# Contiguous one-hot tables, and the weight splits of two experts laid between the row fetches

## Chip, cores and metric

The kernel runs on one core of a Trainium2 chip. The metric is the time of one execution on the device, in microseconds (us). The time before is the median of three runs, 1259.48 us.

## The reference

Two layers run on x of shape (4, 1024, 256), 4096 tokens of 256 features. Each layer is `x = layernorm(x + attention(x))` and then `x = layernorm(x + ffn(x))`. The change touches the last ffn only, a mixture of eight experts of which each token takes two, plus one shared expert:

```python
T = B * S                                   # 4096 tokens, H = 256, D = 512, E = 8
scores = softmax(xt @ Wr)
topk_w, topk_idx = top_k(scores, 2)
topk_w = topk_w / (topk_w.sum(-1, keepdims=True) + 1e-20)
g = silu(einsum('th,ehd->etd', xt, Wg))
u = einsum('th,ehd->etd', xt, Wu)
out_all = einsum('etd,edh->eth', g * u, Wd)
out = sum(out_all[topk_idx, tok] * topk_w[..., None], axis=1)
shared = silu(x @ Sg) * (x @ Su) @ Sd
return out + shared
```

## The kernel before

Matrix products run in pairs of fp32r operands: each fp32 matrix is split in a high part and the rest (low), and a product is three matmuls (function `three`, L1681 to L1683). Each engine's program is written out by hand, with semaphores between them.

The expert stage begins once the tokens are normed. The order of its work is this.

**Routing.** VectorE works out the two experts of each token and, for each of its two places, a slot in a table sorted by expert. The slots form 71 tiles of 128 rows (NE = 71). By the reference's inputs the eight experts take 9, 6, 8, 9, 10, 7, 7 and 12 tiles, so expert 2 begins at tile 15, expert 3 at tile 23, expert 4 at tile 32 and expert 5 at tile 42; three tiles at the end are empty.

**The token table.** Which token stands in slot (tile n, row r) is found by 64 small matmuls (`token_table`, L1993), one for each of 32 blocks of 128 tokens and each of the two places. The stationary operand `in_row` is a one-hot over the 128 rows, the moving operand `in_tile` a one-hot over the 71 tiles, scaled by the token's number. Both are fp16 and are laid out with the block index innermost, eight to a group, so each operand is read at a step of eight elements. VectorE builds `in_tile` (L1549) and `in_row` in four quarters (L1564); ScalarE scales `in_tile` block by block, 32 instructions (L683), each of which releases two matmuls. Between the halves of the table TensorE runs pieces of `down_wide` (L2003), the down projection of the first two chunks of the shared expert. VectorE turns the sums into `token_of` (L1579), and that starts GpSimd.

**GpSimd's queue (L943 to L964).** GpSimd fetches the rows of the first six tiles straight to where TensorE needs them, asks for expert 2's weights (`load_expert(2)`), and fetches the rows of the other 65 tiles in 17 groups. Group 0 is tiles 6 and 7, every other group four tiles (the last three). A `fetch` (L913) is one indirect DMA of 128 rows of 1 KB into one of six stage buffers; `keep` (L920) writes a whole group to DRAM (`tokens_by_expert`), from where ScalarE's queue loads a tile three tiles ahead (L727). Between groups GpSimd splits the weights of experts 2 and 3: `split_expert` copies 128x3072 elements to the high part (L908), drains, and subtracts for the low part (L910), which releases `w_ready`. Slots for weights are three: `load_expert(e)` with e of 3 and more waits until expert e-3 is done with (L935).

**The tile loop.** For each tile TensorE transposes the rows (L2038), runs gate and up (24 matmuls of EWs with xeh, xel), transposes the hidden rows (L2054, four matmuls), and runs down (heh, hel). ScalarE does Silu (L718) and the high parts (L713, L723), VectorE the product (L1625), the low parts (L1619, L1629) and the copy out (L1637), SyncE the store. A tile waits for its rows and, by `w_ready`, for its expert's split weights (L2076).

**The end.** GpSimd gathers the experts' outputs for each token by 64 indirect DMAs (L969), while TensorE runs the other six chunks of the shared expert; then come the last sums and norms.

Of the kernel before, what the change touches and what calls it, by code (L numbers as in the profile page):

```python
# [16 lines left out]
TB = N // P  # L17
KD = D // P
# [8 lines left out]
ROUND = 12582912.0  # L27


C_ID, C_IOTA, C_CAUSAL, C_CHAN = 0, 128, 640, 896  # L30
# [3 lines left out]
C_TOKEN = 1192  # L34
# [14 lines left out]
STAGES = 6  # L49
SLOTS = 3  # L50
AHEAD = 2
# [15 lines left out]
def wait(eng, sem, n):  # L67

    if not isinstance(n, int) or n > 0:
        eng.wait_ge(sem, n)  # L70
# [12 lines left out]
def build(nc, cst, xT, x, wqkvgT, wave_cols, bias_cols, coupling_rows, woutT, bout, wgu_rows, wd_rows, wqk_T, wo_rows, bo, wr, experts, out):  # L83
    ctx = ExitStack()
    with ctx:
        place = {"at": 0, "top": 0}

        def sb(name, shape, dt=F32):
            size = 2 if dt in (BF16, F16) else 4
            for s in shape[1:]:  # L90
                size *= s
            t = nc.alloc_sbuf_tensor_at(name, shape, dt, offset=base + place["at"])
            place["at"] += (size + 31) // 32 * 32
            place["top"] = max(place["top"], place["at"])
            return t

        def sem(name):
            return ctx.enter_context(nc.semaphore(name))
# [3 lines left out]
        PS = ctx.enter_context(nc.psum_tensor("PS", [P, 8, 512], F32))  # L102
# [3 lines left out]
        C = sb("C", [P, C_END])  # L106
# [4 lines left out]
        zrow = sb("zrow", [P, D])  # L111
# [121 lines left out]
        place["at"] = kept  # L233
        in_tile = sb("in_tile", [P, 2, NT // 8, NE, 8], F16)
        inc_ = sb("inc_", [P, NT, E])
# [21 lines left out]
        place["at"] = slot_at + 4 * SLOT  # L257
        in_row = sb("in_row", [P, NT // 8, 2, P, 8], F16)
        posf, tilef = sb("posf", [P, 2, NT]), sb("tilef", [P, 2, NT])
        tile_of, row_of = sb("tile_of", [P, 2, NT], F16), sb("row_of", [P, 2, NT], F16)  # L260
        bigt = sb("bigt", [P, NE + 1, E])
        past, third = sb("past", [P, NE + 1]), sb("third", [P, NE + 1])
        columns = sb("columns", [P, P, 8], F16)
        sco, oh1 = sb("sco", [P, NT, E]), sb("oh1", [P, NT, E])
        assert place["at"] <= slot_at + 8 * SLOT

# [11 lines left out]
        d_gr = [sem("d_gathered" + str(i)) for i in range(NCH)]  # L278
        x_kept, d_tile, d_row, d_token, d_table, d_token_of, d_stage0, d_stage1, d_rows, d_row0, d_row1, d_last = (
            sem("d_" + n) for n in ("x_kept", "tile", "row", "token", "table", "token_of", "stage0", "stage1", "rows", "row0", "row1", "last"))  # L280
        d_stage = (d_stage0, d_stage1)
# [95 lines left out]
        def _(act):  # L377
# [385 lines left out]
        def _(pool):  # L763
# [141 lines left out]
            def split_expert(e):  # L905
# [90 lines left out]
        def _(dve):  # L996
# [447 lines left out]

            dve.tensor_copy(columns[:], C[:, C_IOTA:C_IOTA + P].unsqueeze(2).to_broadcast([P, P, 8]))
            dve.tensor_copy(tri[:], C[:, C_TRI:C_TRI + P])
# [88 lines left out]
            for j, oh in enumerate((oh1, oh2)):  # L1535
                dve.tensor_tensor(tmp[:], slot[:], oh[:], ALU.mult)
                dve.drain()
                dve.tensor_reduce(posf[:, j], tmp[:], AX.X, ALU.add)
                dve.drain()
            dve.tensor_copy(pos[:], posf[:])  # L1540

# [3 lines left out]
            dve.drain()  # L1545
            dve.tensor_scalar(tile_of[:], tilef[:], ROUND, ROUND, ALU.add, ALU.subtract)
            dve.drain()
            dve.scalar_tensor_tensor(row_of[:], tile_of[:], -float(P), posf[:], ALU.mult, ALU.add)
            dve.tensor_tensor(in_tile[:].rearrange("p j q n t -> p (j q) n t"),  # L1549
                              columns[:, 0:NE].unsqueeze(1).to_broadcast([P, NT // 4, NE, 8]),  # L1550
                              tile_of[:].rearrange("p j (q t) -> p (j q) t", t=8).unsqueeze(2).to_broadcast([P, NT // 4, NE, 8]),
                              ALU.is_equal).then_inc(d_tile, 1)
            hidden(1, 2)
            dve.drain()
            def added(c):
                for w in range(2):
                    dve.wait_ge(d_dn, 2 * c + w + 1)
                    rows = X[:, 4 * c + 2 * w:4 * c + 2 * w + 2]
                    src = PS[:, 6 + w].rearrange("p (t d) -> p t d", d=D)
# [8 lines left out]
            added(0)  # L1568
            dve.tensor_scalar(past[:], past[:], float(E - 1), None, ALU.min)
# [8 lines left out]
            dve.wait_ge(d_table, 1)  # L1578
            dve.tensor_scalar(token_of[:], PS[:, 0, 0:NE], float(TOKEN_0), None, ALU.add).then_inc(d_token_of, 1)  # L1579

            def gated(c, part):
# [96 lines left out]
        def _(pe):  # L1678
# [307 lines left out]

            def token_table(first, end):
                for t in range(first, end):
                    pe.wait_ge(d_token, t + 1)
                    if t % (NT // 4) == 0:  # L1990
                        pe.wait_ge(d_row, 4 * t // NT + 1)
                    for j in range(2):
                        mm = pe.matmul(PS[:, 0, 0:NE], in_row[:, t // 8, j, :, t % 8], in_tile[:, j, t // 8, :, t % 8], start=t + j == 0, stop=t + j == NT)  # L1993
                if end == NT:
                    mm.then_inc(d_table, 1)

            def down_wide(c, first, end):
                wait(pe, d_add, 2 * c)
                pe.wait_ge(d_ld, 32)
                for j in range(first, end):  # L2000
                    pe.wait_ge(d_hb, 4 * c + j + 1)
                    for w in range(4):
                        mm = pe.matmul(PS[:, 6 + w // 2, (w % 2) * D:(w % 2 + 1) * D], inner[c][:, j, w * P:(w + 1) * P],  # L2003
                                       wide_down[:, j * D:(j + 1) * D], start=j == 0 and w % 2 == 0, stop=j == 3 and w % 2 == 1)
                        if j == 3 and w % 2:
                            mm.then_inc(d_dn, 1)
# [196 lines left out]
```

## Time and profile before

| | |
|---|---|
| median of 3 runs | 1259.48 us (1257.24 to 1261.27) |
| the profiled execution, its time | 1258.39 us |
| its span in the trace | 1256.2 us |
| TensorE busy | 1068.5 us (85%) |
| VectorE busy | 791.2 us (63%) |
| ScalarE busy | 480.7 us (38%) |
| GpSimd busy | 442.8 us (35%) |

A row of the profile names the line, the engine (PE is TensorE, PEld its weight load, DVE VectorE, ACT ScalarE, POOL GpSimd), the operation, out<-in and the shape. In square brackets is how long the engine stood still before it and what released it. "issue" means that the trace shows nothing that it waited for; "remote" means a queue that the trace does not know. The profiled execution's time lies 2.2 us above its span and 1.1 us below the median.

### The profile page before, as it was taken

The page shows a single profiled execution, that of the slowest core. Times are in us where ns is not written, and L with a number is a line of the kernel's source. Part 1 is how long each engine was busy: PE and PEld are TensorE (multiplying, and loading weights), DVE is VectorE, ACT ScalarE, POOL GpSimd, SP SyncE. Part 2 cuts the span into 40 slices and gives each one's busy share as a digit, 9 for nine tenths or more (in the row PEclk, how much of TensorE's full clock was granted, in tenths as well). Part 3 has the DMA queues.
Part 4 walks back from the last instruction along what each step waited for, and adds up shares of the span by engine and source line. Part 5 has one row for each costly group of instructions (what it writes and reads, how often), then busy time and mean ns, then how long its engine had stood idle before and what let it go on. Part 6 is the DMA issues. An engine that isn't in the chain of part 4 may idle for free.

```text
span 1256.2 us, 19144 instructions
## 1 busy us (share of the span) xinstructions
PE 1068.5 (85%) x5944; PEld 923.8 (74%) x5945; DVE 791.2 (63%) x1337; ACT 480.7 (38%) x813; POOL 442.8 (35%) x387
## 2 busy tenths in 40 slices
PE   5699953599999999999899858699999999832995
PEld 4567733589999998999777747588888888711884
DVE  7978898799999985887652313244444444301887
ACT  6635532234444445667471212123222223200345
POOL 3202003145544454231106767644403000474032
PEclk9989985799999999999999879799999999955998
DMA  6100100000000002112404363651321111232122
GB/s 263 49 20 1 35 41 30 0 2 1 0 0 0 1 1 105 35 34 82 154 1 160 107 225 108 204 159 53 104 100 50 54 54 63 89 104 71 34 85 117
DMA packets 41203, 87.80 MB, mean 70 GB/s; under 512 B 5954, under 2 KB 27716, under 8 KB 39748
## 3 DMA queue, kind: packets, MB, share of 16 engines
q0 software_dynamic: 9696, 35.66, 9.2%
q1 hardware_dynamic: 20660, 39.20, 8.7%
q10 hardware_dynamic: 10800, 12.32, 3.2%
q8 instruction: 28, 0.46, 0.2%
q14 instruction: 19, 0.16, 0.0%
HBM read 57.80 MB, written 29.36 MB: 69 GB/s over the span
## 4 chain that ended last, share of the span: by engine, by line
PE 53%; DVE 15%; DVEq 9%; issue 8%; another core or an unknown queue 8%; ACT 4%; POOL 1%; POOLq 1%; DMA 0%; ACTq 0%
PE PS L1681 14%; PE PS L1683 13%; PE PS L1682 13%; PE PS L2054 3%; PE PS L1805 2%; DVEq L1184 2%; DVEq L1289 2%; ACT in_tile L683 2%; PE PS L1710 2%; DVEq L1301 1%; DVEq L1197 1%; DVE hx L1196 1%; PE PS L2038 1%; PE PS L1723 1%
## 5 line engine op out<-in xcount | busy, mean ns | idle before, releaser
L1625 DVE TENSOR_TENSOR hb<-PS,gs 128x512 f32<-128x512 f32 x71 | 49.1, 691 | 169.1 <-ACT gs L718 155.3
L1681 PE MATMUL PS<-EWs,xeh 128*128 x284 | 122.0, 430 | 1.5 <-DVE xel L1619 1.2
L1682 PE MATMUL PS<-EWs,xeh 128*128 x284 | 114.1, 402 | 0.0
L1683 PE MATMUL PS<-EWs,xel 128*128 x284 | 113.8, 401 | 0.0
L969 POOL DMA_INDIRECT gathered<-expert_outputs,pos x64 | 61.6, 963 | 145.4 <-DMA expert_outputs<-ye 126.1
L718 ACT ACTIVATE gs<-PS 128x512 f32<-128x512 f32 x71 | 42.4, 598 | 177.0 <-PE PS L1683 150.4
L1681 PE MATMUL PS<-WGh,bxh 128*128 128x352 f32 x256 | 88.4, 345 | 19.8 <-DVE hv L1283 13.5
L1681 PE MATMUL PS<-EWs,heh 128*128 x284 | 87.6, 308 | 18.1 <-DVE hel L1629 14.1
L1805 PE MATMUL PS<-WD,htf 128*128 128x256 f32 x384 | 88.5, 380 | 1.6 <-ACT htf L509 1.5
L723 ACT ACTIVATE heh<-PS 128x512 fp32r<-128x512 f32 x71 | 42.5, 598 | 123.2 <-PE PS L2054 90.4
L1682 PE MATMUL PS<-WGl,bxh 128*128 128x352 f32 x256 | 85.6, 334 | 0.0
L1683 PE MATMUL PS<-WGh,bxl 128*128 128x352 f32 x256 | 85.3, 333 | 0.0
L1629 DVE TENSOR_TENSOR hel<-PS,heh 128x512 fp32r<-128x512 f32 x71 | 49.1, 692 | 55.7 <-ACT heh L723 52.5
L1682 PE MATMUL PS<-EWs,heh 128*128 x284 | 81.7, 288 | 0.0
L1683 PE MATMUL PS<-EWs,hel 128*128 x284 | 81.5, 287 | 0.0
L1805 PEld LDWEIGHTS PS<-WD,htf 128*128 128x128 f32 x384 | 71.2, 190 | 10.9 <-ACT htf L509 2.5
L1681 PE MATMUL PS<-DTh,SWh 128*128 128x512 f32 x128 | 53.5, 418 | 20.2 <-issue 13.8
L1681 PE MATMUL PS<-xh,WQh 128*128 128x512 f32 x128 | 53.8, 420 | 19.8 <-DVE WQl L1019 13.2
L1681 PEld LDWEIGHTS PS<-EWs,heh 128*128 128x128 f32 x284 | 55.1, 194 | 19.6 <-issue 19.5
L1681 PEld LDWEIGHTS PS<-EWs,xeh 128*128 128x128 f32 x284 | 55.3, 195 | 17.9 <-issue 2.3
L1681 PEld LDWEIGHTS PS<-WGh,bxh 128*128 128x128 f32 x256 | 50.5, 197 | 23.6 <-issue 14.7
L1683 PE MATMUL PS<-DTh,SWl 128*128 128x512 f32 x128 | 52.4, 409 | 13.8 <-issue 13.8
(359 smaller groups left out, 3063.7 us busy)
## 6 DMA issues: line engine op xcount, KB each, us to landing
raw_of<-experts POOLq DMA_DIRECT2D x6, 1536.0 KB
expert_outputs<-ye SPq DMA_DIRECT2D x71, 128.0 KB
xe<-tokens_by_expert ACTq DMA_DIRECT2D x65, 128.0 KB
xraw<-xT SPq DMA_DIRECT2D x8, 512.0 KB, 5.6
X<-x SPq DMA_DIRECT2D x1, 4096.0 KB, 16.9
tokens<-X SPq DMA_DIRECT2D x8, 512.0 KB, 3.1
y<-X SPq DMA_DIRECT2D x8, 512.0 KB, 2.6
raw_of<-experts SPq DMA_DIRECT2D x2, 1536.0 KB, 9.1
```

The lines of the kernel that those rows point to most:

```text
L683: act.activation(of_t, of_t, ACT.Copy, scale=C[:, C_TOKEN + t:C_TOKEN + t + 1]).then_inc(d_token, 1)
L718: act.activation(gs[:, h], PS[:, 2], ACT.Silu).then_inc(e_si, 1)
L723: act.activation(heh[:, h].rearrange("p a c -> p (a c)"), PS[:, 4 + h], ACT.Copy).then_inc(e_hhi, 1)
L969: pool.indirect_dma_start(out=gathered[c][:, j, t], out_offset=None, in_=YS, in_offset=bass.IndirectOffsetOnAxis(ap=pos[:, j, 4 * c + t:4 ...
L1184: dve.drain()
L1625: dve.tensor_tensor(hb[:, h], PS[:, 3], gs[:, h], ALU.mult).then_inc(e_hb, 1)
L1629: dve.tensor_tensor(hel[:, h].rearrange("p a c -> p (a c)"), PS[:, 4 + h], heh[:, h].rearrange("p a c -> p (a c)").bitcast(F32), ALU.subtr ...
L1681: pe.matmul(out_, wh, vh, start=first, stop=False)
L1682: pe.matmul(out_, wh, vl, start=False, stop=False)
L1683: return pe.matmul(out_, wl, vh, start=False, stop=last_)
L1805: mm = pe.matmul(PS[:, 7, i * D:(i + 1) * D], htf[:, i, k], WD[:, k], start=k == 0, stop=k == FT - 1)
L2054: t = pe.transpose(PS[:, 4 + h, j * P:(j + 1) * P], hb[:, h, j * P:(j + 1) * P], ident)
```

## The change

The tables become contiguous: `in_tile` is [block, place, tile] with 72 columns in place of 71, and `in_row` is [block, place, row]. To keep pairs of equal elements side by side, `tile_of` and `row_of` are written twice each, and the comparison reads the iota row in pairs. ScalarE's 32 scalings go; VectorE multiplies the whole `in_tile` by the token numbers in one instruction ahead of `in_row`. `token_table` runs in one piece between `down_wide(0)` and `down_wide(1)`, which gets banks of its own (4 and 5), and VectorE's `added(0)` moves behind `token_of`.

On GpSimd, the splits of experts 2 and 3 are cut in six column ranges of 512 elements, high and low part each, twelve pieces in all. A piece stands behind every second fetch of groups 2 to 7 (expert 2) and 9 to 14 (expert 3); each low piece has a drain of its own ahead of it. The wait for expert 2's raw weights moves ahead of group 2, the load of expert 3 stays behind group 7, and group 8 goes between it and the wait for it. The splits of experts 4 to 7 stay whole.

```diff
+            def split_part(e, n):
+                place_, half, cols = (e + 2) % SLOTS, n % 2, slice(n // 2 * 2 * D, (n // 2 + 1) * 2 * D)
+                hi, lo, raw = (t[:, cols].rearrange("p (n d) -> p n d", d=D) for t in (hi_of[place_], lo_of[place_], raw_of[place_]))
+                if half == 0:
+                    pool.tensor_tensor(hi, raw, zrow[:, :].unsqueeze(1).to_broadcast([P, 2, D]), ALU.add)
+                else:
+                    pool.drain()
+                    last_ = pool.tensor_tensor(lo, raw, hi.bitcast(F32), ALU.subtract)
+                    if n == PARTS - 1:
+                        last_.then_inc(w_ready, 1)
...
-            def gather_tokens(first, end):
+            def gather_tokens(first, end, split=None):
+                part = 0
                 for g in range(first, end):
...
                     for n, i in enumerate(range(*GROUPS[g])):
                         fetch(stages[g % STAGES][:, n], i, d_stage[g % 2])
+                        if split is not None and n % 2:
+                            split_part(split, part)
+                            part += 1
...
             gather_tokens(0, 2)
             pool.wait_ge(d_dn, 2 * AHEAD)
-            gather_tokens(2, 4)
-            loaded(2)
-            gather_tokens(4, 8)
+            pool.wait_ge(d_raw2, 16)
+            gather_tokens(2, 8, split=2)
             load_expert(3)
-            gather_tokens(8, 10)
-            loaded(3)
-            gather_tokens(10, 16)
+            gather_tokens(8, 9)
+            pool.wait_ge(d_raw2, 16 * 2)
+            gather_tokens(9, 15, split=3)
+            gather_tokens(15, 16)
             load_expert(4)
...
-            act.wait_ge(d_tile, 1)
-            for t in range(NT):
-                of_t = in_tile[:, :, t // 8, :, t % 8]
-                act.activation(of_t, of_t, ACT.Copy, scale=C[:, C_TOKEN + t:C_TOKEN + t + 1]).then_inc(d_token, 1)
...
+            dve.tensor_tensor(each_tile, pairs(columns[:, 0:NE + 1], 2 * NT), doubled(tile_of[:], (NE + 1) // 2), ALU.is_equal)
             hidden(1, 2)
             dve.drain()
+            dve.tensor_tensor(each_tile, each_tile, doubled(tokens[:].rearrange("p t (j d) -> p t j d", d=2), (NE + 1) // 2),
+                              ALU.mult).then_inc(d_tile, 1)
...
-                dve.tensor_tensor(in_row[:, q], columns[:].unsqueeze(1).to_broadcast([P, 2, P, 8]),
-                                  row_of[:, :, 8 * q:8 * q + 8].unsqueeze(2).to_broadcast([P, 2, P, 8]), ALU.is_equal).then_inc(d_row, 1)
+                dve.tensor_tensor(in_row[:, 8 * q:8 * q + 8].rearrange("p t j (n d) -> p (t j) n d", d=2), pairs(columns[:], 16),
+                                  doubled(row_of[:, 8 * q:8 * q + 8], P // 2), ALU.is_equal).then_inc(d_row, 1)
...
-            down_wide(0, 0, 4)
-            token_table(0, NT // 2)
-            down_wide(1, 0, 1)
-            token_table(NT // 2, NT)
-            down_wide(1, 1, 4)
+            down_wide(0)
+            token_table()
+            down_wide(1)
```

## Rows read from the trace of the kernel before

**Rows 1.** Busy time by stretch: from, to, length; busy us (instructions), clock, DMA share, GB/s.

```profile
713.80:756.90 43.10, 27.47 (x139) 23.22 (x139) 10.42 (x20) 7.15 (x15) 28.57 (x32) 0.79 0.64 201
756.90:773.30 16.40, 16.40 (x92) 13.92 (x91) 5.88 (x13) 4.42 (x9) 13.58 (x2) 0.92 0.22 72
773.30:811.00 37.70, 24.71 (x114) 20.21 (x112) 8.22 (x16) 5.39 (x11) 27.05 (x30) 0.77 0.59 181
811.00:833.00 22.00, 20.79 (x125) 17.96 (x125) 8.97 (x17) 5.88 (x12) 12.03 (x8) 1.00 0.61 180
833.00:913.00 80.00, 80.00 (x477) 69.12 (x476) 33.51 (x63) 23.55 (x48) 35.40 (x9) 1.00 0.27 90
```

**Rows 2.** TensorE's tile transposes between 668.9 and 832.8 us, grouped by line.

```profile
L2054 PE MATMUL PS<-C,hb 128*128 128x128 f32 x92 | 17.0, 314 | 17.9 <-issue 11.1 <-DVE hb L1625 6.8
```

**Rows 3.** Timeline, TensorE and GpSimd, end of the gather stage.

```profile
1125.32 0.59 PE L1681 MATMUL PS<-DTh,SWh 128*128 128x512 f32 x1 [2.21 <-issue]
...
1149.44 0.94 POOL L969 DMA_INDIRECT gathered<-expert_outputs,pos  x1 [0.30 <-issue]
...
1155.42 0.59 PE L1683 MATMUL PS<-DTh,SWl 128*128 128x512 f32 x1 [1.51 <-issue]
```

**Rows 4.** TensorE in order of time, token table, first tile and tile 23.

```profile
638.04 0.39 PE L1682 MATMUL PS<-DTl,SWh 128*128 128x512 f32 x1
638.27 0.40 PE L1683 MATMUL PS<-DTh,SWl 128*128 128x512 f32 x1
638.50 7.07 PE L2003 MATMUL PS<-wide_down,inner 128*128 128x256 f32 x32
...
650.18 3.51 PE L2003 MATMUL PS<-wide_down,inner 128*128 128x256 f32 x8
...
660.48 7.11 PE L2003 MATMUL PS<-wide_down,inner 128*128 128x256 f32 x24
...
668.99 0.50 PE L1681 MATMUL PS<-EWs,xeh 128*128 x1 [1.18 <-DVE xel L1619]
...
832.90 0.50 PE L1681 MATMUL PS<-EWs,xeh 128*128 x1
```

**Rows 5.** The table's instructions: duration ns (min/median/max), first and last start.

```profile
L1993 PEld LDWEIGHTS PS<-in_tile,in_row x64: 142/145/171, 645.2 to 660.2; 128*128 128x128 f16 x64
```

**Rows 6.** VectorE in order of time, table building.

```profile
636.10 2.52 DVE L1549 TENSOR_TENSOR in_tile<-columns,tile_of 128x4544 f16<-128x4544 f16 x1
641.05 3.49 DVE L1564 TENSOR_TENSOR in_row<-columns,row_of 128x2048 f16<-128x2048 f16 x3
660.69 0.23 DVE L1579 TENSOR_SCALAR token_of<-PS 128x71 int32<-128x71 f32 x1 [13.15 <-PE PS L1993]
```

**Rows 7.** GpSimd in order of time, from group 2 to expert 3's split.

```profile
682.94 1.01 POOL L913 DMA_INDIRECT Hh<-tokens,token_of  x1 [0.30 <-issue]
...
706.86 6.79 POOL L910 TENSOR_TENSOR EWs<-raw_of,EWs 128x3072 fp32r<-128x3072 f32 x1 [2.21 <-issue]
713.81 1.04 POOL L913 DMA_INDIRECT Hl<-tokens,token_of  x1 [0.16 <-issue]
...
724.74 0.99 POOL L913 DMA_INDIRECT even_rows<-tokens,token_of  x1 [0.30 <-issue]
...
730.60 0.97 POOL L913 DMA_INDIRECT even_rows<-tokens,token_of  x1 [0.30 <-issue]
...
741.01 0.56 POOL L937 DMA_DIRECT2D raw_of<-experts  x1 [0.30 <-issue]
...
756.91 6.78 POOL L908 TENSOR_TENSOR EWs<-raw_of,zrow 128x3072 fp32r<-128x3072 f32 x1
```

**Rows 8.** GpSimd in order of time, around experts 4 and 5.

```profile
812.36 0.56 POOL L937 DMA_DIRECT2D raw_of<-experts  x1 [0.30 <-issue]
...
834.50 6.82 POOL L910 TENSOR_TENSOR EWs<-raw_of,EWs 128x3072 fp32r<-128x3072 f32 x1 [3.02 <-issue]
...
855.22 6.80 POOL L910 TENSOR_TENSOR EWs<-raw_of,EWs 128x3072 fp32r<-128x3072 f32 x1 [0.24 <-issue]
```

More of the change, by code:

```diff
@@ L257, in build @@
         place["at"] = slot_at + 4 * SLOT
-        in_row = sb("in_row", [P, NT // 8, 2, P, 8], F16)
-        posf, tilef = sb("posf", [P, 2, NT]), sb("tilef", [P, 2, NT])
-        tile_of, row_of = sb("tile_of", [P, 2, NT], F16), sb("row_of", [P, 2, NT], F16)
+        in_row = sb("in_row", [P, NT, 2, P], F16)
+        posf, tilef = sb("posf", [P, NT, 2]), sb("tilef", [P, NT, 2])
+        tile_of, row_of = sb("tile_of", [P, NT, 2, 2], F16), sb("row_of", [P, NT, 2, 2], F16)
         bigt = sb("bigt", [P, NE + 1, E])
         past, third = sb("past", [P, NE + 1]), sb("third", [P, NE + 1])
-        columns = sb("columns", [P, P, 8], F16)
+        columns = sb("columns", [P, P], F16)
         sco, oh1 = sb("sco", [P, NT, E]), sb("oh1", [P, NT, E])
+        tokens = sb("tokens", [P, NT, 4], F16)
         assert place["at"] <= slot_at + 8 * SLOT
@@ L278, in build @@
         d_gr = [sem("d_gathered" + str(i)) for i in range(NCH)]
-        x_kept, d_tile, d_row, d_token, d_table, d_token_of, d_stage0, d_stage1, d_rows, d_row0, d_row1, d_last = (
-            sem("d_" + n) for n in ("x_kept", "tile", "row", "token", "table", "token_of", "stage0", "stage1", "rows", "row0", "row1", "last"))
+        x_kept, d_tile, d_row, d_table, d_token_of, d_stage0, d_stage1, d_rows, d_row0, d_row1, d_last = (
+            sem("d_" + n) for n in ("x_kept", "tile", "row", "table", "token_of", "stage0", "stage1", "rows", "row0", "row1", "last"))
         d_stage = (d_stage0, d_stage1)
@@ L1443, in every, with pairs, doubled, twice @@
                 return v.unsqueeze(1).to_broadcast([P, NT, E])
-            dve.tensor_copy(columns[:], C[:, C_IOTA:C_IOTA + P].unsqueeze(2).to_broadcast([P, P, 8]))
+            def pairs(v, n):
+                return v.rearrange("p (n d) -> p n d", d=2).unsqueeze(1).to_broadcast([P, n, v.shape[1] // 2, 2])
+            def doubled(v, n):
+                return v.rearrange("p t j d -> p (t j) d").unsqueeze(2).to_broadcast([P, v.shape[1] * 2, n, 2])
+            def twice(v):
+                return v.rearrange("p t j -> p (t j)").unsqueeze(2).to_broadcast([P, 2 * NT, 2])
+            dve.tensor_copy(columns[:], C[:, C_IOTA:C_IOTA + P])
+            dve.tensor_copy(tokens[:], C[:, C_TOKEN:C_TOKEN + NT].unsqueeze(2).to_broadcast([P, NT, 4]))
             dve.tensor_copy(tri[:], C[:, C_TRI:C_TRI + P])
@@ L1545, in _ @@
             dve.drain()
-            dve.tensor_scalar(tile_of[:], tilef[:], ROUND, ROUND, ALU.add, ALU.subtract)
+            dve.tensor_scalar(tile_of[:].rearrange("p t j d -> p (t j) d"), twice(tilef[:]), ROUND, ROUND, ALU.add, ALU.subtract)
             dve.drain()
[L1548 to L1552, printed above, removed]
+            dve.scalar_tensor_tensor(row_of[:].rearrange("p t j d -> p (t j) d"), tile_of[:].rearrange("p t j d -> p (t j) d"), -float(P),
+                                     twice(posf[:]), ALU.mult, ALU.add)
+            each_tile = in_tile[:].rearrange("p t j (n d) -> p (t j) n d", d=2)
+            dve.tensor_tensor(each_tile, pairs(columns[:, 0:NE + 1], 2 * NT), doubled(tile_of[:], (NE + 1) // 2), ALU.is_equal)
             hidden(1, 2)
             dve.drain()
+            dve.tensor_tensor(each_tile, each_tile, doubled(tokens[:].rearrange("p t (j d) -> p t j d", d=2), (NE + 1) // 2),
+                              ALU.mult).then_inc(d_tile, 1)
             def added(c):
@@ L1558, in added @@
                     rows = X[:, 4 * c + 2 * w:4 * c + 2 * w + 2]
[L1559 removed]
+                    src = PS[:, (4 if c == 1 else 6) + w].rearrange("p (t d) -> p t d", d=D)
                     dve.tensor_tensor(rows, src, rows, ALU.add).then_inc(d_add, 1)
@@ L1579, in _ @@
             dve.tensor_scalar(token_of[:], PS[:, 0, 0:NE], float(TOKEN_0), None, ALU.add).then_inc(d_token_of, 1)
+            added(0)
             def gated(c, part):
@@ L1985, in places, with token_table @@
                 pe.matmul(PS[:, 1, 0:NT * E], ones[:], ohr[:], start=True, stop=True).then_inc(d_pre, 1)
-            def token_table(first, end):
-                for t in range(first, end):
-                    pe.wait_ge(d_token, t + 1)
+            def token_table():
+                pe.wait_ge(d_tile, 1)
+                for t in range(NT):
                     if t % (NT // 4) == 0:
@@ L1992, in token_table, with down_wide @@
                     for j in range(2):
[L1993 to L1998, printed above, removed]
+                        mm = pe.matmul(PS[:, 0, 0:NE], in_row[:, t, j], in_tile[:, t, j, 0:NE], start=t + j == 0, stop=t + j == NT)
+                mm.then_inc(d_table, 1)
+            def down_wide(c):
+                bank = 6 - 2 * c
                 pe.wait_ge(d_ld, 32)
-                for j in range(first, end):
+                for j in range(4):
                     pe.wait_ge(d_hb, 4 * c + j + 1)
                     for w in range(4):
-                        mm = pe.matmul(PS[:, 6 + w // 2, (w % 2) * D:(w % 2 + 1) * D], inner[c][:, j, w * P:(w + 1) * P],
+                        mm = pe.matmul(PS[:, bank + w // 2, (w % 2) * D:(w % 2 + 1) * D], inner[c][:, j, w * P:(w + 1) * P],
                                        wide_down[:, j * D:(j + 1) * D], start=j == 0 and w % 2 == 0, stop=j == 3 and w % 2 == 1)
```

8 lines of the change are left out of this document (4 added, 4 removed).

## The prediction

> **What bounds the kernel now.** I read the page first, for the busy shares, and then the stretch of the tile loop in windows, the timelines of TensorE, GpSimd and VectorE through it, and the operands of the token table by tile. The page says that TensorE is the busiest engine, at 85% of the span. The windows show where it isn't [rows 1]: from 833 to 913 us it does 477 matmul records in 80 us, 5.96 per us, at full clock. In 713.8 to 756.9 it does 139 in 43.1 us (3.2 per us), in 773.3 to 811 it does 114 in 37.7 (3.0 per us); both are stretches in which GpSimd issues row fetches back to back. In 756.9 to 773.3, with GpSimd at a split, it does 92 in 16.4 (5.6 per us). The volume of the DMAs isn't what slows it: in 811 to 833 they are as busy (0.61 against 0.59) and TensorE does 5.7 per us; there GpSimd makes three fetches, one weight load and a split.
>
> Tile 0 starts its gate product at 668.99 [rows 4] and 92 transposes, 23 tiles, later comes tile 23 at 832.90 [rows 2, 4]. That is 163.9 us for 23 tiles; at the later pace of 16 tiles in 80 us [rows 1], 5.0 each, it would be 115. So 48.9 us are lost, nearly all while fetches run. How it looks closely is plainest in the gather at the end, where GpSimd issues 56 indirect DMAs in a row: TensorE takes one matmul every 0.59 + 2.21 = 2.80 us and waits for nothing that the trace shows [rows 3]. I have no cause for this, only the company it keeps, and call it the crawl. Behind tile 23 the loop goes at full pace up to its end, so that what moves tile 23 moves the end as far.
>
> Ahead of the loop, the path is one of waits: the table's last matmul, `token_of` at 660.69 [rows 6], the rest of `down_wide`, tile 0.
>
> **The table.** VectorE's added product has 64 x 72 = 4608 fp16 elements; the comparison of 4544 such took 2.52 us [rows 6], so 2.6 us. It stands before `in_row`, whose last quarter ended at 641.05 + 3.49 = 644.5 and now ends at 647.1. ScalarE's 32 scalings, the last of which held the table to 660.4, go, and nothing else waited in ScalarE's queue. TensorE starts the table at 645.2 [rows 5], behind `down_wide(0)`, as before; the tables for its first half are ready by then. Its 64 weight loads took 142 to 145 ns each [rows 5]: 9.2 us and an end at 654.4 if laying them out contiguously does nothing. From below: a matmul of 512 columns follows the last at 0.23 us [rows 4], 0.44 ns a column, so 128 columns 57 ns and 64 loads 3.6 us, an end at 648.8. I take 0.1 us each, between them: 6.4 us, end 651.6, `token_of` done some 0.5 us later, as before, at 652.1 in place of 660.92. Gain 8.8 us (6.0 to 11.6). The doubled `tile_of` and `row_of` add some 0.1 us in front, hidden as TensorE isn't yet through `down_wide(0)`.
>
> The rows [rows 5] show loads read at a step of 16 bytes at 142 ns, 2.5 times the 57 ns. The Trainium skill speaks on both sides. "TensorE: Matmul & The Clock Gate" (Weight-path perf modes — Fast Weight Load (FWL) and DoubleRow) has the fast load of weights that aren't fp32 work "packed or strided"; by that contiguity brings nothing and `token_of` ends at 654.9. "SBUF — State Buffer" has a penalty for each access that crosses to a new 16-byte line; by that the step was what cost, and the end lies near 649. The trace, which has no contiguous fp16 load, bears out neither.
>
> Then all 16 products of `down_wide(1)` follow: 6.9 us as in `down_wide(0)`, or up to 10.3 if the clock is at half at their start, as it was for the four that took 3.51 us [rows 4]. With 8.7 us, and the 1.4 us that lay from the end of `down_wide` to tile 0, tile 0 starts at 662: 7 us earlier (4 to 9).
>
> **GpSimd's chain.** It starts 8.8 us earlier. From `token_of`'s end to group 2's first fetch it is 682.94 - 660.92 = 22.0 us, unchanged. Expert 2's raw weights, asked for 9.5 us in, should be there. One group of four fetches and a store takes 730.60 - 724.74 = 5.86 us [rows 7]. To this come two pieces: a sixth of 6.80 us is 1.13, with a gap of 0.16 [rows 7] 1.29 each, 2.6 us. And a drain. The whole split's drain took 2.2 us soon after a store and 3.0 once, but 0.24 with no store near [rows 7, 8]; now it stands behind two fetches, once a group. No row shows that; I take 1.0 (0.24 to 3.0), nearer to the low end since a fetch gives 128 rows and a store 512. A group then takes 9.4 us (8.7 to 11.5).
>
> Group 7's first fetch comes five groups less one store later, 46.2 us; from there to the load of expert 3 it was 10.4 us [rows 7] and is 14.0 with the pieces and the drain: 82.2 us after `token_of`. From that load to the split it was 15.9 us with two groups, with one 10.0: group 9 begins at 92.2. The last low piece ends 46.2 + 8.4 us on, at 146.8, which is 652.1 + 146.8 = 798.9 us. Split 3, which was 60 us early for tile 23, is now the last to come: TensorE without any crawl would be at tile 23 at 662 + 115 = 777.
>
> Expert 2 is hidden: its last piece ends 22 + 46.2 + 8.4 = 76.6 after `token_of`, 728.7, and tile 15 isn't before 662 + 75 = 737. Expert 4 is hidden by some 5 us: from 798.9 it takes 0.2 + 5.0 + 5.7 us to its load, and 29.0 from there to the end of its split [rows 8], 838.8, against tile 32 at 798.9 + 45. Rows are no bound: four tiles take TensorE 20 us and GpSimd 9.4.
>
> **The sum.** Tile 23 starts at 798.9, not 832.9: 34.0 us. I take off 2 us for the fetches of groups 15 and 16, which still stand back to back and now lie behind tile 23: 32. The profiled execution's 1258.4 less 32 is 1226.4, and the median, 1.1 above that execution, is 1227.
>
> This rests on TensorE being at tile 23 by 799, so on no more than 22 us of crawl where there were 48.9. Why I think so: fetches now come at 9.4/4 = 2.35 us each on average in place of 1.46. And the crawl outlasts the last of the 56 gathers, issued 1.25 us apart, by some 5 us [rows 3]. That looks like a surplus that piles up, of 5 us over 70, and is then worked off. A third fewer fetches per us would keep it from piling up.
>
> **The rivals.**
> *The crawl goes by the fetch, not by their density*, or the drains are all 3 us. Then the same fetches cost the same 49 us: tile 23 at 662 + 164 = 826; or the pieces take 11.5 us a group and the split ends 25 us later, at 824. Either gives some 7 to 9 us: 1251. For it speaks that nobody knows the cause; against it, that three fetches in 811 to 833 cost next to nothing [rows 1].
> *Slower: the pieces don't interrupt the run.* GpSimd's fetch stage is now one run from 662 to some 816, where it had two whole splits as pauses of 16 us in which TensorE went at full pace. If TensorE keeps the burst's 3.1 records per us, 53% of full pace, from 685 on, it does 131 x 0.53 / 5.0 = 13.9 tiles in it after 3.5 before, and tile 23 starts at 816 + 5.6 x 5.0 = 844: 11 us later, 1270. It decides from a pace below 60% in the stage. For it: a store stands behind every fourth fetch already, 5.86 - 4 x 1.25 = 0.86 us [rows 7], and the two bursts crawl all the same; a piece is 1.29.
> *Nothing changes*: a mixture of these that lands on 1259.
>
> **The numbers.** I give the forecast 0.57, the first rival 0.19, the slower one 0.16, and nothing 0.08. The likeliest's own range is 1215 (8.7 us a group and the table at its lower bound, 43 us) to 1243. Over all: 1215 to 1261, which leaves out most of the slower rival and the extremes. Within 0.3% (3.8 us) is about what a measurement of this kernel can't tell from no change: faster 0.77, same 0.07, slower 0.16.
>
> **What would show it.** Right: weight loads of the table nearer 0.06 than 0.14 us and `token_of` at about 652; group periods near 9.4 us on GpSimd with drains near 1 us; TensorE above 5 records per us while pieces and fetches alternate; before tile 23 a wait of TensorE for the last low piece at about 799; full pace after. Wrong: TensorE with the 53% pace and unexplained waits in that stage, no wait for the weights at tile 23, or drains of 3 us.

## The result, and the profile after

The changed kernel takes 1241.51 us (1238.56 to 1243.37, four runs) where the kernel before takes 1258.36 beside it (1256.10 to 1261.27, four runs): a ratio of 0.9863, 95% interval 0.9831 to 0.9894. That is 17 us faster; 32 were forecast, in a range of 1215 to 1261. The profiled execution has a span of 1241.3 us, against 1256.2.

Stretches of the changed kernel, with the columns of [rows 1]: fetches with pieces of expert 2's split, fetches with pieces of expert 3's, the wait before tile 23, the 80 us behind it, and part of the gathers at the end:

```profile
670.00:735.00 65.00, 63.46 (x382) 54.65 (x380) 27.87 (x53) 19.13 (x39) 41.75 (x41) 1.00 0.47 142
740.00:776.70 36.70, 36.61 (x220) 31.46 (x220) 16.03 (x31) 10.38 (x22) 22.79 (x25) 1.00 0.58 186
776.70:813.70 37.00, 0.29 (x3) 0.06 (x1) 0.88 (x2) 0.60 (x1) 24.83 (x25) 0.53 0.32 99
813.70:893.70 80.00, 78.07 (x454) 67.12 (x455) 31.38 (x60) 22.09 (x45) 49.88 (x23) 0.98 0.45 143
1080.00:1130.00 50.00, 13.05 (x27) 6.55 (x25) 0.00 (x0) 0.00 (x0) 37.95 (x40) 0.53 0.37 105
```

The first two lines answer the bursts of [rows 1], 3.2 and 3.0 records per us: it is 5.9 and 6.0 now, full pace, with fetches and pieces alternating. The crawl is gone there. The third line is what took its place: TensorE does nothing for 37 us. The last shows that the crawl at the end is as it was, 27 records in 50 us. The kernel before, in a stretch of the same length:

```profile
1095.00:1145.00 50.00, 14.06 (x27) 7.16 (x27) 0.00 (x0) 0.00 (x0) 37.81 (x41) 0.52 0.36 105
```

TensorE in order of time, from `down_wide(0)` to tile 0, then at tiles 15 and 23:

```profile
640.03 7.07 PE L2026 MATMUL PS<-wide_down,inner 128*128 128x256 f32 x32
646.94 2.48 PE L2017 MATMUL PS<-in_tile,in_row 128*128 128x71 f16 x64
649.25 7.15 PE L2026 MATMUL PS<-wide_down,inner 128*128 128x256 f32 x32
656.24 0.38 PE L2061 MATMUL PS<-C,xe 128*128 128x128 f32 x2
657.81 0.49 PE L1705 MATMUL PS<-EWs,xeh 128*128 x1 [1.18 <-DVE xel L1643]
...
736.13 0.49 PE L1705 MATMUL PS<-EWs,xeh 128*128 x1 [2.29 <-POOL EWs L917]
...
813.80 0.79 PE L1705 MATMUL PS<-EWs,xeh 128*128 x1 [36.81 <-POOL EWs L917]
```

Tile 0 starts at 657.81 and not at 668.99 [rows 4], 11.2 us earlier, tile 23 at 813.80 and not at 832.90, 19.1 us earlier; the brackets name the last low piece of experts 2 and 3. The start of tile 0 varies from one profiled execution to the next, whatever stands at the table: 651.1 to 658.9 in the ten with the new table, 664.0 to 669.0 in the four with the old. Their means, 655.6 and 667.5, lie 11.9 us apart, so the 11.2 is no accident. The table's 64 products take 2.48 us in all. Their weight loads, with the columns of [rows 5]:

```profile
L2017 PEld LDWEIGHTS PS<-in_tile,in_row x64: 96/100/102, 646.7 to 649.2; 128*128 128x128 f16 x64
```

VectorE in order of time, answering [rows 6]:

```profile
637.73 2.55 DVE L1574 TENSOR_TENSOR in_tile<-columns,tile_of 128x4608 f16<-128x4608 f16 x1
...
640.97 2.56 DVE L1577 TENSOR_TENSOR in_tile<-in_tile,tokens 128x4608 f16<-128x4608 f16 x1
...
645.18 3.48 DVE L1588 TENSOR_TENSOR in_row<-columns,row_of 128x2048 f16<-128x2048 f16 x3
...
649.83 0.23 DVE L1602 TENSOR_SCALAR token_of<-PS 128x71 int32<-128x71 f32 x1
```

GpSimd in order of time, answering [rows 7]: one group with its two pieces, the load of expert 3, the end of its split.

```profile
682.51 0.97 POOL L922 DMA_INDIRECT Hh<-tokens,token_of  x1
683.79 0.95 POOL L922 DMA_INDIRECT Hh<-tokens,token_of  x1 [0.30 <-issue]
684.75 1.30 POOL L914 TENSOR_TENSOR EWs<-raw_of,zrow 128x512 fp32r<-128x512 f32 x1
686.21 0.96 POOL L922 DMA_INDIRECT Hh<-tokens,token_of  x1 [0.16 <-issue]
687.48 0.95 POOL L922 DMA_INDIRECT Hh<-tokens,token_of  x1 [0.30 <-issue]
690.84 1.29 POOL L917 TENSOR_TENSOR EWs<-raw_of,EWs 128x512 fp32r<-128x512 f32 x1 [2.41 <-issue]
692.07 0.80 POOL L929 DMA_DIRECT2D tokens_by_expert<-Hh  x1
693.17 1.00 POOL L922 DMA_INDIRECT Hl<-tokens,token_of  x1 [0.30 <-issue]
...
740.99 0.56 POOL L950 DMA_DIRECT2D raw_of<-experts  x1 [0.29 <-issue]
...
812.15 1.26 POOL L917 TENSOR_TENSOR EWs<-raw_of,EWs 128x512 fp32r<-128x512 f32 x1 [2.09 <-issue]
```

A group takes 693.17 - 682.51 = 10.66 us. The drain is the 2.41 us of idle time ahead of the low piece. All twelve, in GpSimd's instructions grouped by line and shape from 660 to 815 us (the last number is idle time ahead of them):

```profile
L914 POOL TENSOR_TENSOR EWs<-raw_of,zrow 128x512 fp32r<-128x512 f32 x12 | 15.5, 1293 | 0.3
L917 POOL TENSOR_TENSOR EWs<-raw_of,EWs 128x512 fp32r<-128x512 f32 x12 | 15.3, 1278 | 29.4 <-issue 29.4
```

That is 29.4 us in twelve drains: 2.45 each, where 1.0 was taken.

### The profile page after: what moved, and what is told of

It is laid out like the page before. It is cut to its first block, busy times and chain, and to the rows that moved or that the text cites. A ratio compares the mean times of both kernels' runs of the same rounds, so it can differ in the third digit from the quotient of the medians.

```text
span 1241.3 us, 19142 instructions
## 1 busy us (share of the span) xinstructions
PE 1045.4 (84%) x5944; PEld 906.8 (73%) x5945; DVE 793.1 (64%) x1339; ACT 459.9 (37%) x781; POOL 448.3 (36%) x407
## 4 chain that ended last, share of the span: by engine, by line
PE 47%; DVE 15%; issue 14%; DVEq 10%; POOL 8%; POOLq 2%; ACT 2%; DMA 1%; ACTq 0%
PE PS L1705 13%; PE PS L1707 12%; PE PS L1706 12%; PE PS L1829 2%; PE PS L2077 2%; DVEq L1197 2%; DVEq L1302 2%; PE PS L1734 1%; POOL even_rows L922 1%; POOL EWs L914 1%; DVEq L1314 1%; DVEq L1210 1%; POOL EWs L917 1%; DVE hx L1209 1%; POOLq L916 1%
## 5 line engine op out<-in xcount | busy, mean ns | idle before, releaser
L1705 PE MATMUL PS<-EWs,xeh 128*128 x284 | 119.4, 420 | 40.3 <-POOL EWs L917 39.1
L1706 PE MATMUL PS<-EWs,xeh 128*128 x284 | 111.4, 392 | 0.0
L1705 PE MATMUL PS<-EWs,heh 128*128 x284 | 85.7, 302 | 1.5 <-DVE hel L1653 1.5
L1706 PE MATMUL PS<-EWs,heh 128*128 x284 | 80.1, 282 | 0.0
L1705 PEld LDWEIGHTS PS<-WGh,bxh 128*128 128x128 f32 x256 | 50.4, 197 | 23.8 <-issue 14.9
L1706 PE MATMUL PS<-DTl,SWh 128*128 128x512 f32 x128 | 52.9, 413 | 13.3 <-issue 13.2
```

Of the source, the lines that this page charges most:

```text
L1705: pe.matmul(out_, wh, vh, start=first, stop=False)
L1706: pe.matmul(out_, wh, vl, start=False, stop=False)
```

## The experiments

There are twelve experiments, on four chips; the fifth repeats the changed kernel, the last two repeat the first two. The kernel before was timed beside each: 1254 to 1258 us on three of the chips, 1161.27 (1159.53 to 1165.48, nine runs) on the fourth, on which the first four experiments ran. Ratios are to the kernel before on the same chip. All runs on one chip were made together, so what is said below of a chip may also be its state at that time.

**1. The new table alone**: the changed kernel with the old calls on GpSimd.

```diff
-            pool.wait_ge(d_raw2, 16)
-            gather_tokens(2, 8, split=2)
+            gather_tokens(2, 4)
+            loaded(2)
+            gather_tokens(4, 8)
             load_expert(3)
-            gather_tokens(8, 9)
-            pool.wait_ge(d_raw2, 16 * 2)
-            gather_tokens(9, 15, split=3)
-            gather_tokens(15, 16)
+            gather_tokens(8, 10)
+            loaded(3)
+            gather_tokens(10, 16)
```

> The changed kernel with GpSimd's old order: expert 2's and 3's splits whole again, the new token table kept. Theory (the two edits are two links of one chain, and the crawl depends on how GpSimd's fetches follow each other): token_of ends 11 to 12 us earlier, tile 0 starts near 658, the crawl costs its 49 us before tile 23 as in the kernel before, tile 23 near 822, whole time 1258.4 - 11 = 1247. Rival (the crawl is gone for another reason than the pieces, for instance because the table's tiles or ScalarE's products are gone): 23 tiles in about 119 us, tile 23 near 777 to 785, whole time below 1215.

1153.65 us beside 1161.27, ratio 0.9929 (0.9908 to 0.9950). Neither expectation was made for such a chip: with the old bursts of fetches, TensorE goes from tile 0 at 655.70 to tile 23 at 772.70, 117.0 us where [rows 4] have 163.9. Its windows in a burst of fetches and in the gathers:

```profile
662.00:700.00 38.00, 38.00 (x232) 33.11 (x230) 15.79 (x31) 11.18 (x23) 25.99 (x17) 1.00 0.45 150
1050.00:1110.00 60.00, 60.00 (x334) 52.51 (x333) 49.38 (x104) 20.70 (x32) 46.87 (x46) 1.00 0.44 131
```

6.1 and 5.6 records per us: no crawl in either place, with the same instructions on GpSimd. TensorE waits 10.5 us for expert 4's split instead. The table alone gains 7.6 us there.

**2. The new order alone**: the opposite edit, on the kernel before.

> The kernel before with GpSimd's new order alone, the old table kept. Theory: token_of at 660.9 as before, tiles of 5.0 to 5.1 us while pieces and fetches alternate, expert 3's last low piece 163.4 us behind token_of as in the changed kernel, at 824.3, and TensorE waits for it before tile 23, which starts 8 us earlier than the 832.9 before; some 4 us of it are lost behind tile 23, so 1258.4 less 4 to 8: 1250 to 1254. Rival (pieces and table help each other): no change at all, 1258, or slower.

On this chip 1191.11 us, ratio 1.0241 (1.0208 to 1.0275), 30 us slower. Tile 23 starts at 823.01 (824 expected), after this wait (TensorE's waits from 657 to 870 us: total, times, longest):

```profile
PE PS L1697 <- POOL EWs L920: 38.1, 2, 36.8
```

So the new order comes at a price of its own, a wait at tile 23 of the same size on each chip (36.2 to 36.8 us in four executions). What it buys is the end of the crawl, and where there is none, it buys nothing.

**3. The drains away**: a semaphore from each high piece to its low piece.

```diff
-                    pool.tensor_tensor(hi, raw, ..., ALU.add)
+                    pool.tensor_tensor(hi, raw, ..., ALU.add).then_inc(p_hi, 1)
                 else:
-                    pool.drain()
+                    pool.wait_ge(p_hi, (e - 2) * PARTS // 2 + n // 2 + 1)
```

> The changed kernel, with each low piece waiting for its high piece by a semaphore in place of the drain. Theory (the drain waits for the fetches' descriptors, 2.45 us twelve times): the period of four fetches falls from 10.6 to 8.2 us, expert 3's last low piece ends 12 x 2.4 = 29 us earlier, at about 784, the load of expert 3 isn't held by its wait for tile 8, and TensorE's wait before tile 23 shrinks from 36.8 to about 8 us; whole time 1241.5 - 27 = 1214. First rival (the time in the drains was what let TensorE keep its pace): fetches now come at 2.0 us each, the crawl returns in part, tiles take over 5.5 us, tile 23 later than 795, whole time 1225 to 1240. Second rival (the drain's time is work that GpSimd owes anyway): the pieces or the next fetches grow by as much, period stays 10.6 us, 1241.

1151.64 us beside 1161.27, ratio 0.9912 (0.9885 to 0.9940). GpSimd, second and third group:

```profile
677.34 0.97 POOL L922 DMA_INDIRECT Hh<-tokens,token_of  x1 [0.16 <-issue]
...
683.25 1.30 POOL L917 TENSOR_TENSOR EWs<-raw_of,EWs 128x512 fp32r<-128x512 f32 x1
684.48 0.80 POOL L929 DMA_DIRECT2D tokens_by_expert<-Hh  x1
685.59 1.00 POOL L922 DMA_INDIRECT Hl<-tokens,token_of  x1 [0.30 <-issue]
```

8.25 us a group (8.2 expected); the last low piece ends at 782.2 (784 expected) and the wait at tile 23 is 10.1 us in place of some 37. A group took 10.6 us with the drain, so a drain costs 10.6 - 8.25 = 2.35 us of the chain, and neither the pieces nor the fetches grew when it went: the second rival is refuted. The first couldn't be told here, as this chip has no crawl.

**4. Breaks between the gathers**: an idle addition behind every second of the 64 gathers at the end.

```diff
                                                 ).then_inc(d_gr[c], 16)
+                        if (2 * t + j) % 2 == 1:
+                            pool.tensor_tensor(rest[:], ..., ALU.add).then_inc(p_rest, 1)
```

> The changed kernel, with an idle addition of 128x512 zeros on GpSimd (1.3 us, into a buffer that nobody reads) behind every second of the 64 gathers at the end, where TensorE does 0.4 matmul records per us for 60 us. Nothing else is changed. Theory (the crawl is a surplus that piles up while GpSimd issues indirect DMAs 1.25 us apart, and pauses work it off): TensorE keeps above 4 records per us through the gathers, which now come 2.0 us apart and end near 1205; the shared expert's work lies beside them; whole time 1225 (1215 to 1235). Rival (a cost of each gather, whatever stands between): TensorE does 0.4 to 0.6 records per us for as long as gathers run, now 128 us, the end 46 us later, 1287. Second rival (it goes by density in proportion): crawl weaker, 1 to 3 records per us, end within 15 us of 1241.

1211.18 us, ratio 1.0421, on the chip without a crawl: it says nothing of the crawl, only what breaks cost where none are needed. The ratio holds the price of the new order too. The changed kernel wasn't timed on this chip; from experiments 1 and 2 I estimate it at 1161.27 x 0.9929 x 1.0241 = 1181 us, which leaves some 30 us for 32 additions of 1.05 us. The last gather was issued at 1182.94.

**5. The changed kernel itself**, on another chip (before: 1253.63).

> The changed kernel itself, unaltered, because the kernel before took 1161.3 us on the chip that ran the first four experiments and not 1258.4: there the crawl was missing altogether. Theory (the crawl belongs to the chip or to its state at the time, the split's delay to the kernel): if the kernel before takes about 1161 here, TensorE runs 23 tiles in 115 us, waits 36 to 37 us for expert 3's last low piece at tile 23, and the changed kernel takes 1161 + 16 = 1177, slower by some 1.3%; if the kernel before takes about 1258, it takes 1241 as in the first comparison. Rival (the change is worth the same 17 us everywhere): 1144 beside 1161.

1239.87 us, ratio 0.9868 (0.9811 to 0.9925), the first result over again. The wait before tile 23 is 36.2 us, tile 23 starts at 810.37.

**6. Earlier loads**, with the semaphores of experiment 3.

```diff
-            gather_tokens(2, 8, split=2)
+            gather_tokens(2, 7, split=2)
             load_expert(3)
-            gather_tokens(8, 9)
+            gather_tokens(7, 8, split=2, part=PARTS - 2)
             pool.wait_ge(d_raw2, 16 * 2)
-            gather_tokens(9, 15, split=3)
-            gather_tokens(15, 16)
+            gather_tokens(8, 13, split=3)
             load_expert(4)
-            gather_tokens(16, len(GROUPS))
+            gather_tokens(13, 14, split=3, part=PARTS - 2)
+            gather_tokens(14, len(GROUPS))
```

> The changed kernel with the semaphore in place of the drains, and with the load of expert 3 behind group 6 and not 7, its pieces from group 8 on and not 9, and the load of expert 4 before group 13. Theory (the wait at tile 23 is GpSimd's order alone): expert 3's last low piece ends near 770, ahead of tile 23; no wait of over 1 us of TensorE in the loop; beside a kernel before of 1161, 10 us less than the variant with the semaphore alone: 1141. Beside one of 1258 the crawl decides: 1200 to 1215. Rival (the early load is held by its wait for expert 0's last tile, or its transfer for the fetches): the wait goes to tile 15, 1150.

1216.86 us beside 1253.63, ratio 0.9693 (0.9626 to 0.9759): 23 us less than the changed kernel beside it, and 2 us above the range expected (1200 to 1215). TensorE's windows:

```profile
680.00:720.00 40.00, 40.00 (x240) 34.59 (x239) 16.82 (x32) 11.77 (x24) 31.61 (x33) 1.00 0.60 185
720.00:760.00 40.00, 40.00 (x238) 34.35 (x237) 16.60 (x33) 11.63 (x24) 32.80 (x32) 1.00 0.57 186
```

6.0 records per us without a drain, on a chip that crawls: the first rival of experiment 3 falls as well. The time in the drains isn't what kept TensorE going. The last low piece ended at 779.65 and not at 770, because each call of `gather_tokens` ends with a store that waits for its own fetches, and the new cuts at the two loads and at group 8 made that 3.42 + 2.15 + 3.18 = 8.8 us of idle time on GpSimd. A wait of 7.8 us at tile 23 remains. With the semaphores alone it was 10.1 (experiment 3, on the other chip), so the early loads brought little beyond them.

**7. A break behind every fourth gather**, otherwise the changed kernel.

> The changed kernel with the idle addition behind every fourth of the 64 gathers at the end (not every second). If the kernel before takes about 1161 here, TensorE keeps its pace in the gathers anyway, and the 16 additions of 1.2 us only make the gathers end later: 0 to 20 us above the changed kernel beside it. If it takes about 1258, TensorE does 0.4 records per us in the gathers without the additions: then theory (a surplus that piles up) expects over 4 records per us and 1241 less 20 to 40, the rival (a cost of each gather) 1241 plus 16 or more.

1192.65 us (one run), 47 us less than the changed kernel beside it, more than the 20 to 40 expected. TensorE in the gathers:

```profile
1070.00:1130.00 60.00, 55.54 (x328) 49.11 (x327) 52.21 (x87) 19.03 (x29) 50.00 (x48) 1.00 0.37 110
```

328 records in 60 us, against 27 in 50. GpSimd in order of time:

```profile
1081.41 0.95 POOL L983 DMA_INDIRECT gathered<-expert_outputs,pos  x1 [0.30 <-issue]
1082.66 1.16 POOL L983 DMA_INDIRECT gathered<-expert_outputs,pos  x1 [0.30 <-issue]
1083.84 1.05 POOL L991 TENSOR_TENSOR rest<-zrow 128x512 f32<-128x512 f32 x1
1085.05 0.97 POOL L983 DMA_INDIRECT gathered<-expert_outputs,pos  x1 [0.16 <-issue]
```

One addition of 1.05 us makes four gathers take about 6.2 us in place of 5.0; part of that is that a gather itself takes 1.04 us on average here and 0.96 in the kernel before. "A cost of each gather" is out. Breaks do it, or the lower rate that comes with them: no run spaces the gathers evenly at 1.55 us, so these two aren't told apart.

**8. The same break with an addition of 128x16.**

> The changed kernel with an idle addition of 128x16 zeros on GpSimd behind every fourth of the 64 gathers at the end, in place of the 128x512 that took the crawl out of them (1192.7 beside 1239.9). Only told apart where the kernel before takes about 1250. Theory 1 (what counts is the time that GpSimd issues nothing): this addition takes 0.1 us and not 1.05, four gathers 5.3 us and not 6.2, the crawl stays, 1235 to 1245. Theory 2 (what counts is that an instruction other than a DMA stands between them): the crawl is gone, TensorE over 5 records per us in the gathers, 1185 to 1195, or less since the gathers end 15 us earlier.

1230.32 us (one run) beside 1257.79, where 1241 was the changed kernel's. The addition took 0.23 us, most of it in the 0.30 us that lies between two gathers anyway: four gathers now take 1083.69 - 1078.57 = 5.12 us, not 5.0. Its window in the gathers:

```profile
1080.00:1120.00 40.00, 5.03 (x15) 3.36 (x14) 3.56 (x6) 1.23 (x2) 31.59 (x40) 0.58 0.36 103
```

15 records in 40 us: TensorE is held up as before, though by two long stops rather than by many short ones:

```profile
1103.77 0.80 PE L1713 MATMUL PS<-DTh,SWh 128*128 128x512 f32 x1 [23.07 <-issue]
1135.30 0.80 PE L1713 MATMUL PS<-DTh,SWh 128*128 128x512 f32 x1 [27.19 <-DVE hb L1636]
```

That another instruction stands between isn't enough; the time without an issue counts. The 11 us under the changed kernel, from one run on another chip, I leave unexplained.

**9. The kernel before with breaks only**: an addition of 128x384 behind each group's fetches, table and splits as they were.

```diff
                         fetch(stages[g % STAGES][:, n], i, d_stage[g % 2])
+                    pause()
                     if g > first:
                         keep(g - 1)
```

> The kernel before, its table and its whole splits unaltered, with an idle addition of 128x384 zeros on GpSimd (about 0.8 us) behind each group's row fetches, ahead of the store. Where the kernel before takes about 1250: theory (short breaks take the crawl out, the splits needn't be what makes them): tile 0 at 669, tile 23 at 669 + 115 = 784 and not 833, then some 10 us of wait for expert 4's split, so 1254 less 39 is 1215. Rival (the crawl goes by how many fetches per us, and 6.8 us for four are still too dense): tile 23 after 815, 1235 to 1254. Where the kernel before takes about 1161: nothing to win, groups 1 us longer, 1161 to 1166.

1233.65 us beside 1257.79, ratio 0.9808 (0.9778 to 0.9839). The two stretches in which [rows 1] had the first burst, then expert 3's split with the second:

```profile
713.80:756.90 43.10, 37.81 (x223) 31.82 (x222) 15.83 (x30) 10.42 (x22) 32.60 (x36) 1.00 0.63 196
756.90:799.40 42.50, 37.20 (x210) 31.30 (x208) 15.16 (x29) 10.31 (x21) 32.82 (x24) 0.96 0.41 128
```

5.2 and 4.9 records per us: tile 23 starts at 799.43 and not at 832.90, tile 0 at 668.0. An addition of 0.83 us makes a group 734.92 - 728.25 = 6.67 us in place of 5.86 and takes two thirds of the 49 us away; 799.4 - 668.0 - 115 = 16 stay. That lies between theory (784) and rival (after 815), as does the time. Of the 33 us, 9 are lost again behind tile 23 (432.6 us to the end of the span, 423.3 before), 4.0 of them in a wait for expert 4's split. Breaks alone, with the old table, gain 24 us, about what the whole change does or a little more.

**10. All of it together**: experiments 3 and 6, breaks behind each group without pieces and behind every fourth gather.

> The changed kernel with all that helped put together: semaphores in place of the drains, the loads of experts 3 and 4 earlier, an idle addition of 128x384 zeros behind each group of row fetches that has no pieces, and one behind every fourth gather at the end. Where the kernel before takes about 1254: the early loads gave 23 us beside the changed kernel and the breaks in the gathers 47, so 1240 - 70 = 1170; with the last bursts of fetches freed too, 1160. Where it takes about 1161: no crawl to take out, the order gives 20 us, the breaks in the gathers cost 0 to 15: 1141 to 1156. Rival (a break comes at a price that shows once the crawl is gone, since the last chunks wait for later gathers): above 1180 or above 1161.

1164.00 us (1160.19 to 1165.23, four runs) beside 1257.79, ratio 0.9246 (0.9214 to 0.9279): faster than both kernels, about what the kernel before takes on the chip without a crawl, and close to the 1160 expected. TensorE in the gathers:

```profile
1060.00:1120.00 60.00, 56.29 (x320) 48.57 (x318) 50.08 (x97) 17.41 (x27) 49.26 (x50) 1.00 0.39 119
```

It hasn't been timed on that chip.

**11 and 12. Table alone and order alone again**, on a chip that crawls (before: 1256.50).

> The new table with GpSimd's old order once more, since the first time it met a chip on which the crawl was missing (before 1161.3). Where the kernel before takes about 1255: theory: token_of 11 us earlier, everything behind it as in the kernel before, the crawl of some 49 us included, tile 23 near 822 and the whole 11 us less, ratio 0.991; the rest of the changed kernel's 17 us, some 6, is what the pieces bring once their wait of 36 us is paid out of the crawl's 49. Rival (the crawl comes and goes by itself): ratio anywhere between 0.96 and 1.01.

> GpSimd's new order with the old table once more. Where the kernel before takes about 1255: theory: no crawl before tile 23, a wait of some 36 us for expert 3's last low piece at 824, tile 23 near 825 and not 833, less what is lost behind it: ratio 0.994 to 0.998. Rival (pieces are worth more than that by themselves): below 0.99.

Table alone: 1247.61 us, ratio 0.9923 (0.9900 to 0.9947), tile 23 at 820.68 (822 expected). Order alone: 1249.41 us, 0.9947 (0.9926 to 0.9967), a wait of 36.7 us, tile 23 at 818.70 (825 expected, but tile 0 had started 5 us earlier in this execution). The product of the two is 0.987, the ratio of the whole change. The table alone in a burst of fetches:

```profile
662.00:700.00 38.00, 33.96 (x186) 29.23 (x185) 12.74 (x25) 8.74 (x18) 26.87 (x17) 0.91 0.44 144
```

It is to be held against the same stretch of the same kernel on the chip without a crawl (experiment 1): 186 records for 232, with 17 instructions of GpSimd in both.

## Why the prediction was right, and where it was off

**The direction and the mechanism held.** Crawl out, split of expert 3 in as the new bound, tile 23 set by its last low piece: the chain forecast is the one that the trace shows. Experiments 2 and 12 show its wait, experiment 3 that it shrinks by what is taken out of GpSimd's chain.

**The crawl was costed rightly.** At most 22 of the 48.9 us were to stay; from tile 0 to tile 22, which starts at 771.74, 22 tiles took 113.9 us, 2.9 of it lost at tile 15, so 5.05 each: one us stayed. The reason given, a surplus that pauses work off, agrees with experiments 7, 8 and 9: 1.2 us more for four gathers clear it, 0.8 us more for four fetches and a store clear two thirds, 0.12 us don't. That there is such a surplus is not shown. The slower rival, that pieces don't interrupt the run, has its opposite shown. Its time was also too high by its own terms: from 662 to 685 us there is room for 4.6 tiles and not 3.5, which gives 1265 and not 1270.

**The term that was mis-sized is the drain**: "I take 1.0 (0.24 to 3.0), nearer to the low end since a fetch gives 128 rows and a store 512". It took 2.45, 2.35 of them net. Twelve times 1.35 is 16.2 us, and the last low piece came 813.41 - 650.06 = 163.4 us behind `token_of` where 146.8 was forecast, 16.6 later. The row that resembled it most was the drain soon after a store, 2.2 us [rows 7]; what was reasoned about rows per DMA had no row behind it. The pieces were 1.29 us for 1.13, net 1.2 each (half of 8.25 - 5.86), near the 1.29 summed. The drains also put the run closer to the first rival than to the forecast: with drains of 3 us the last low piece was to come 171.9 us behind `token_of`, 8.5 after the measured one. The time still fell within the forecast's own range, partly since the table gave more.

**The table gave more than was taken**: `token_of` at 650.06 and not at 652.1, tile 0 at 657.81 and not at 662. The loads lie 2.5 / 63 = 0.04 us apart (0.1 taken, 0.057 as the lower bound), at a duration of 100 ns in place of 145; the table began at 646.9 and not at 645.2, which took 1.7 us of that back. And `down_wide(1)` ran in 7.15 us, at full clock, where 8.7 was taken. Contiguity paid. The clock isn't what did it: the loads at a step came 0.136 us apart (28 in 3.81 us) at a granted clock of 1.00, the contiguous ones 0.04 at 1.00. But both operands became contiguous at once, so the share of each isn't known. Of the two rules weighed, the trace speaks against reading the fast load of the Trainium skill ("TensorE: Matmul & The Clock Gate", Weight-path perf modes — Fast Weight Load (FWL) and DoubleRow) so that a step of 16 bytes costs nothing, and agrees with the Trainium skill's "SBUF — State Buffer" (Door 1: The DMA port swizzle), where each access that crosses to a new line of 16 bytes pays. The step of 16 bytes and the contiguous layout were timed, other steps weren't.

**Expert 2 wasn't hidden**: its last piece ended at 735.74 and not at 728.7, six drains at 1.35 us more each, less 2.0 for the earlier `token_of`, and tile 15 waited 2.29 us.

**Behind tile 23** 4.2 us were lost (427.5 to the end of the span, 423.3 before), for 2 forecast. Part of it is a start at half clock (0.53 in the third window), at which the first matmuls took 0.63 us each instead of 0.40: the first six take from 813.80 to 816.53, 2.7 us, where six at full clock take 1.4. The rest I put to the late fetches; no run shows it by itself.

The sum by measured terms: 19.1 - 4.2 = 14.9 us between the two spans, 16.9 between the medians. Of the 32 forecast, 16 went into drains.

**What the prediction did not know** is that its crawl is no property of the kernel. On a chip without it the new order by itself costs 30 us (experiment 2) and the table gains 7.6, so that the change would most likely be slower there; it wasn't timed on that chip.

## What to carry to other kernels

Cutting a long job into pieces between DMA issues costs more than the pieces: ask what each piece must wait for, and let it wait on a semaphore of its own producer and not on a drain, which cost 2.35 us each behind two fetches. When an edit seems to work because it breaks up a run of DMA issues, try the break alone: one idle microsecond in four gathers was worth 47 us (one run), nearly three times the whole change. And find out whether the loss that an edit removes is there on every chip, before paying for the removal.

## What the runs showed of the hardware that was not expected

TensorE's crawl beside indirect DMAs issued 1.25 us apart is there on three of the four chips of the experiments and absent on one, with the same instructions on GpSimd: 186 against 232 records in one stretch of fetches, 97 us of the whole time. In the gathers the rates differ a little (36 in 45 us with the crawl, 46 in 60 without), in the fetches they don't. Where the crawl is, TensorE's releases, the semaphore updates that tell other engines of a finished product, come late too. In experiment 5 this is ScalarE's longest wait from 1040 to 1150 us:

```profile
ACT gs L695 <- remote: 66.0, 1, 66.0
```

The last matmul of the product that it waits for starts at 1104.08; the trace's semaphore events have its release at 1139.93, 35.9 us later. Releases of matmuls at 1076.07 and 1082.29 come at 1137.68 and 1139.81, 61.6 and 57.5 us later. All of them stand behind the end of the gathers, of which the last in the trace is issued at 1130.31. The stop of 27.19 us in experiment 8 is such a chain as well: TensorE waits for VectorE, which waits for ScalarE, whose longest wait there, 32.7 us, is for a product of TensorE. As a rule TensorE's release follows the start of its matmul by 0.29 to 0.41 us. In the first burst of experiment 11 it is 3 to 12 us, several times over; on the chip without a crawl there is one such delay from 640 us on, 5.97. Some records are missing from a trace, and one that is missing looks like a delay of one tile, 5 us, so single figures of this size are uncertain. The 35.9 and 61.6 are not of that kind. Whether TensorE is slow because its releases are late, or both have one cause, is not shown. The cause stays open, and what differs between the chips wasn't in reach. Every timed run here was recorded by the profiler, so none shows whether the recording has a part. The Trainium skill, "NOTIFIC — the notification-queue block" (Overflow: three behaviours, one of which stalls the engine), says that a full queue of records can hold up its engine; no run here shows that.

A drain of GpSimd behind two fetches took 2.09 to 3.43 us, as long as one behind a store (2.21 and 3.02 [rows 7, 8]). Weight loads of fp16 at a step of 16 bytes took 142 to 171 ns, half of them 145 or less; contiguous ones took 96 to 102 and overlapped to 40 ns apart.
